# Loading x in two parts and the later weights after the first stage, in a two-layer cross-attention and feed-forward kernel

## The reference

```
x = x + L0_xattn(layernorm(x), ctx, ctx, ...)     # 16 heads of 16, softmax over 375 keys
x = x + L0_ffn(layernorm(x), ...)                 # 32 routed experts + 8 empty ones, top 6 of 40
x = x + L1_xattn(layernorm(x), ctx, ctx, ...)
x = x + L1_ffn(layernorm(x), ...)                 # gate, up, down, weights and inputs rounded to fp4 by blocks of 16
```

## Time and profile before

| | |
|---|---|
| runs | 1001.34, 998.26, 998.67 us; median 998.67 |
| profiled execution | 1005.61 us, of which the span of instructions 1003.8 us |
| TensorE busy | 898.1 us (89%) |
| VectorE busy | 626.4 us (62%) |
| ScalarE busy | 437.4 us (44%) |
| GpSimd busy | 304.1 us (30%) |
| mean granted TensorE clock | 0.951 of full |
| DMA | 90.45 MB, mean 90 GB/s |

### The profile page before, as it was taken

How to read it: one execution, slowest core, us unless ns; L and a number is a source line. 1 busy time by engine, 2 the same in 40 slices (tenths; PEclk the granted TensorE clock), 3 DMA queues, 4 the chain that set the end, 5 groups by cost and what they waited for, 6 DMA issues and landing times.

```text
span 1003.8 us, 19829 instructions
## 1 busy us (share of the span) xinstructions
PE 898.1 (89%) x7228; PEld 685.1 (68%) x7228; DVE 626.4 (62%) x1317; ACT 437.4 (44%) x946; POOL 304.1 (30%) x311
## 2 busy tenths in 40 slices
PE   2997799999997978999999967799999996699996
PEld 1764687878876747878888844587878874366664
DVE  3455577878854594545545465566777764678872
ACT  0442466666664561111111112466666675345442
POOL 8003466767782260000000004000000001476673
PEclk9998799999998798999999977999999999999998
DMA  9788644444333469121111204345565500000000
GB/s 258 219 238 203 113 93 92 93 93 93 62 106 98 138 214 250 46 67 32 32 32 48 65 3 82 74 85 112 107 117 109 106 27 21 0 11 16 16 10 22
DMA packets 98157, 90.45 MB, mean 90 GB/s; under 512 B 43554, under 2 KB 85410, under 8 KB 97954
## 3 DMA queue, kind: packets, MB, share of 16 engines
q1 hardware_dynamic: 98066, 89.25, 36.6%
HBM read 69.36 MB, written 19.63 MB: 89 GB/s over the span
## 4 chain that ended last, share of the span: by engine, by line
PE 72%; DVE 12%; DMA 5%; POOL 3%; ACT 3%; issue 2%; SPq 2%; DVEq 0%; POOLq 0%; ACTq 0%
PE ps L988 13%; PE ps L805 8%; PE ps L859 8%; PE ps L791 8%; PE ps L994 7%; PE ps L819 7%; PE ps L1062 3%; DMA Qz<-mT 3%; PE ps L709 3%; PE ps L1078 2%; PE ps L868 2%; POOL Pr L645 2%; PE ps L779 2%; PE ps L828 1%; DMA X<-x_in 1%
## 5 line engine op out<-in xcount | busy, mean ns | idle before, releaser
L1444 DVE TENSOR_REDUCE ext<-ps 112x2 f32<-112x750 f32 x256 | 232.6, 933 | 66.5 <-PE ps L791 63.4
L1175 ACT ACTIVATE Pr<-ps 125x448 f32<-125x448 f32 x384 | 199.2, 542 | 88.5 <-PE ps L805 75.0
L805 PE MATMUL ps<-Qz,Kp 98*125 98x224 f16 x768 | 130.7, 265 | 14.0 <-DMA Qz<-mT 11.7
L791 PE MATMUL ps<-Kp,Qz 96*112 96x375 f16 x512 | 122.6, 332 | 5.8 <-DMA Qz<-qscr 4.9
L805 PEld LDWEIGHTS ps<-Qz,Kp 98*125 98x125 f16 x768 | 94.8, 137 | 47.2 <-DMA Qz<-mT 15.9
L859 PE MATMUL ps<-wv,ctx 128*125 128x256 f32 x384 | 120.7, 400 | 1.9 <-DVE xT L1417 1.0
L599 POOL TENSOR_TENSOR X<-X,bo 112x256 f32 x32 | 22.5, 724 | 284.6 <-DVE Pr L1362 233.0
L1585 DVE TENSOR_TENSOR Pr<-Pr,ps 128x336 f32<-128x336 f32 (+2 forms) x86 | 32.7, 381 | 88.9 <-ACT Pr L1257 73.8
L819 PE MATMUL ps<-Pr,Vx 125*32 125x112 f32 x3072 | 86.9, 261 | 0.0
L819 PEld LDWEIGHTS ps<-Pr,Vx 125*32 125x32 f32 x3072 | 71.4, 110 | 14.9 <-ACT Pr L1175 10.3
L1589 DVE SCALAR_TENSOR_TENSOR X<-ps,W,X 112x256 f32<-112x256 f32 x167 | 70.7, 477 | 17.3 <-PE ps L994 17.3
(11 more groups left out here) (176 smaller groups left out, 1417.1 us busy)
## 6 DMA issues: line engine op xcount, KB each, us to landing
ctx<-ctxT SPq DMA_DIRECT2D x56, 375.0 KB, 3.7
Kp<-kscr SPq DMA_DIRECT2D x96, 187.5 KB, 4.8
kscr<-ksp SPq DMA_DIRECT2D x24, 375.0 KB, 4.2
Pr<-wexp SPq DMA_DIRECT2D x20, 384.0 KB, 4.2
Qz<-qscr SPq DMA_DIRECT2D x174, 28.0 KB, 4.1
expert<-wexp SPq DMA_DIRECT2D x12, 384.0 KB, 3.9
Pr<-ctxT SPq DMA_DIRECT2D x8, 375.0 KB, 4.5
kscr<-Pr SPq DMA_DIRECT2D x8, 375.0 KB, 3.9
```

What stands on the lines that cost most here:

```text
L791: last = mm(ps[0:S, 2 * (p % 2) + u, 0:M], Qz[0:96, q0 + u * S:q0 + (u + 1) * S], Kp[0:96, k0:k0 + M], start=True, stop=True)
L805: last = mm(ps[0:KC, 4 + k % 2, u * 2 * S:(u + 1) * 2 * S], Kp[0:98, k0:k0 + KC], Qz[0:98, q0:q0 + 2 * S], start=True, stop=True)
L1175: A(Pr[g % 2][0:KC, j, GI * t:GI * t + GI, :].rearrange("r h q -> r (h q)"), ps[0:KC, 4 + k % 2, 0:GI * S], ACT.Exp, scale=scale).then_inc ...
L1444: V.tensor_reduce(ext[0:S, 2 * p:2 * p + 2], ps[0:S, 2 * (p % 2):2 * (p % 2) + 2, 0:M], AX_X, red).then_inc(row_maximum_taken, 1)
```

## The change

- SP first issues the key weights and biases of layer 0, context 0, a quarter of x (4 sequences, 448 KB), context 1, the query weights, the rest of x (12 sequences, 1,344 KB), and the four other loads of layer 0.
- The other 15 loads (3,327 KB) are issued once, right after `flatten(0)` of layer 0, the `fq` weights first.
- TensorE and ScalarE start on key weights and biases alone. TensorE waits for the query weights before its first query projection.
- VectorE computes statistics of 4 sequences, normalises three, then waits for the rest of x and computes the statistics of the other 12, and only then enters the loop with `split_low(0)`.
- `scale_weights` runs one sequence later: nothing at b = 0, piece b - 1 at b, and both of the last two pieces at b = 15. The wait for `fq` moves from the first row maximum to b = 1.
- Readers of the layer-1 and router weights wait for `late_weights_loaded`.

```diff
-        NW0, NW = 16 * 3, 16 * (4 + 7 + 3)
+        NWK, NW, NL = 16 * 2, 16 * 4, 16 * (7 + 3)
+        XA = 4
...
             weight(wk[0], attn[0]["wk"], first_weights_loaded)
+            sp.dma_start(bqk[0][:, :], attn[0]["bqk"]).then_inc(first_weights_loaded, 16)
             load_ctx(0, 0)
-            sp.dma_start(X[:, :], x).then_inc(x_loaded, 16)
-            weight(wq[0], attn[0]["wq"], first_weights_loaded)
-            sp.dma_start(bqk[0][:, :], attn[0]["bqk"]).then_inc(first_weights_loaded, 16)
+            sp.dma_start(X[:, 0:XA * D], x[:, 0:XA * D]).then_inc(x_loaded, 16)
             load_ctx(1, 1)
-            for l in (0, 1):
...
+            weight(wq[0], attn[0]["wq"], query_weights_loaded)
+            sp.dma_start(X[:, XA * D:], x[:, XA * D:]).then_inc(x_rest_loaded, 16)
...
+            load_attention_weights(0, weights_loaded)
+
+            def load_late_weights():
+                for n, w in enumerate((fg, fu)):
+                    sp.dma_start(fq[:, 6 * D * n:6 * D * n + 5 * D].rearrange("p (t d) -> p t d", d=D),
+                                 w[0:640, :].rearrange("(t p) d -> p t d", p=128)).then_inc(ffn_weights_loaded, 16)
+                    sp.dma_start(fq[0:64, 6 * D * n + 5 * D:6 * D * (n + 1)], w[640:704, :]).then_inc(ffn_weights_loaded, 16)
+                sp.dma_start(fq[:, 12 * D:12 * D + 2 * FI].rearrange("p (t d) -> p t d", d=FI),
+                             fd.rearrange("(t p) d -> p t d", p=128)).then_inc(ffn_weights_loaded, 16)
+                weight(wq[1], attn[1]["wq"], late_weights_loaded)
+                weight(wk[1], attn[1]["wk"], late_weights_loaded)
+                sp.dma_start(bqk[1][:, :], attn[1]["bqk"]).then_inc(late_weights_loaded, 16)
+                load_attention_weights(1, late_weights_loaded)
+                sp.dma_start(wc_sb[:, :, :], wc.rearrange("(c p) o -> p c o", p=128)).then_inc(late_weights_loaded, 16)
+                sp.dma_start(eb_sb[:, :], ebias.partition_broadcast(128)).then_inc(late_weights_loaded, 16)
+                sp.dma_start(pow_sb[:, :], powers).then_inc(late_weights_loaded, 16)
...
                 flatten(0)
+                if l == 0:
+                    load_late_weights()
...
-                norms(False, 0, B if l == 0 else QG)
+                norms(False, 0, XA if l == 0 else QG)
...
                     layer_norm(2, xn[0]).then_inc(x_normalised, 1)
-                    dve.wait_ge(first_weights_loaded, NW0)
+                    dve.wait_ge(first_weights_loaded, NWK)
+                    dve.wait_ge(x_rest_loaded, 16)
+                    norms(False, XA, B)
...
-                if l == 0:
-                    dve.wait_ge(ffn_weights_loaded, 16 * 5)
-                    dve.wait_ge(padding_set, 7)
...
-                        elif step == "q" and l == 0:
-                            scale_weights(b, next(steps))
+                        elif step == "q" and l == 0 and b > 0:
+                            k = next(steps)
+                            if b == 1 and k == 0:
+                                dve.wait_ge(ffn_weights_loaded, 16 * 5)
+                                dve.wait_ge(padding_set, 7)
+                            scale_weights(b - 1, k)
+                            if b == B - 1 and k == 2:
+                                for k in range(3):
+                                    scale_weights(B - 1, k)
```

More of the change, by code:

```diff
@@ L215, in build @@
         first_weights_loaded = sem("first_weights_loaded")
+        query_weights_loaded = sem("query_weights_loaded")
+        late_weights_loaded = sem("late_weights_loaded")
+        x_rest_loaded = sem("x_rest_loaded")
         x_loaded = sem("x_loaded")
@@ L397, in _, with load_attention_weights @@
-            sp.dma_start(fq[:, 12 * D:12 * D + 2 * FI].rearrange("p (t d) -> p t d", d=FI),
-                         fd.rearrange("(t p) d -> p t d", p=128)).then_inc(ffn_weights_loaded, 16)
+            weight(wq[0], attn[0]["wq"], query_weights_loaded)
+            sp.dma_start(X[:, XA * D:], x[:, XA * D:]).then_inc(x_rest_loaded, 16)
+            def load_attention_weights(l, done):
+                weight(wv[l], attn[l]["wv"], done)
+                weight(wo[l], attn[l]["wo"], done)
+                sp.dma_start(bv_sb[l][:, :], attn[l]["bv"]).then_inc(done, 16)
+                sp.dma_start(bo_sb[l][:, :], attn[l]["bo"].partition_broadcast(128)).then_inc(done, 16)
```

25 lines of the change are left out of this document (7 added, 18 removed).

## The result

The changed kernel takes **1015.9 us** (median of 4 runs, 1014.5 to 1017.4), beside 1000.0 for the kernel before on the same chip: ratio 1.0156, interval 1.0124 to 1.0188. The forecast was 1000.7 with a range to 1004.5, so the kernel is slower by 1.6%, and outside the range.

What follows compares the result with a forecast made beforehand. The prediction took TensorE to hold most of the chain of waits, except through the first 30 us. Its terms, -5.4 + 2.8 + 2.4 + 2.2 = +2.0, gave 1000.7 us for the median, range 994.6 to 1004.5.

Steps and rivals of the forecast that it cites:

- Term 1: The start: third sequence's keys 8.1 us earlier, less 2.7 for a cold clock; -5.4 us (ends -7.5 and -3.5).
- term 4: Router's root chain: GpSimd's quantising, a sequence later, holds VectorE's short links; +2.2 us (0.8 to 3.4).
- the start doesn't do what it says: Rival at the start: the rest of x lands at 16.6, sum +3.6, 1002.3 us; chance 0.10.
- Term 2: Queue at `flatten(1)`: its few bytes wait behind the late loads, delaying sequence 1's columns; +2.8 us (0.5 to 5.9).
- SyncE's rival: Queue at `flatten(1)`: the 15 issues stall as at the start; sum +5.7, 1004.4 us; chance 0.15.
- Term 3: TensorE's clock behind the 3.8 us gap at sequence 1's columns falls to half; +2.4 us (0 to 3.05).
- Edits at nothing: Waits for `fq` and other late weights, and VectorE's three short instructions moved to b = 15, cost nothing.

Runs made afterwards that it cites:

- start_scale_late: start_alone with the scales of the expert weights computed one sequence later; ratio 1.0032 to the kernel before.
- start_alone: The kernel before with only the new start (x in two loads, two sets of statistics), late loads and scales in their old places; ratio 1.0020.
- after_spread: The changed kernel with five late loads kept behind `flatten(0)` and the ten others behind the flattenings of sequences 1 to 4; 1.0061 of the kernel before.
- late_alone: The kernel before with only the moved late loads and later scales, keeping the old start; ratio 1.0114.
- start_ctx_first: start_alone with 32-bit memsets, the keys' one after the third normalisation, and sequence 2's context ahead of the late loads; 0.9936 of the kernel before.
- after_memset_cover: The changed kernel with GpSimd's memsets as 32-bit words, the keys' one waiting until the third sequence is normalised; 1.0066 of the kernel before.

## Why the prediction was wrong, point by point

**Term 1, -5.4 us; it was +3.9.** This is the step that failed, and in it the sentence "the first quarter of x no longer matters: its statistics and the first two sequences are done before the rest is". I timed the early chain by its undisturbed links, while GpSimd's memset of 10.09 us stood in the trace of before at just that time, 10.71 to 20.80. I used the very mechanism in term 4, on GpSimd's 1.61 us instructions. I did not ask it of the place to which the chain was moved, where a link of 0.17 us took 10.12. The Trainium skill, page "SBUF — State Buffer", section "Who interferes with whom", says that whichever of VectorE and GpSimd takes their shared ports first holds them for its whole instruction, and names `tensor_scalar` among the VectorE instructions that can want them. The trace agrees: the held links of the start are `tensor_scalar`, and `bn_stats` beside the same memset kept 0.33 us. The arithmetic from the landing of the rest of x was right: with the memset away, 25.20 against 24.1, and 5.8 us against 5.4. The rival "the start doesn't do what it says" had a late x as its cause, at 0.10 and up to +3.6. Its sign was right, its cause wrong: the rest of x landed at 15.3 to 16.2 where it could be seen. Of the 3.9 us, 1.7 are the clock at the third keys, and that part is not sure to come: TensorE was idle 2.93 us there and restarted at 1.2 GHz, but with nearly the same start it was idle 2.82 in start_scale_late and 2.39 in start_alone and stayed at 2.4. (A slip beside it: the lower end of the term, -7.5, comes out of its own figures as -7.1, for a landing at 13.5 and 2.5 of clock.)

**Term 2, +2.8; it was +4.9.** The wait was the one I named, and the fifteen issues took 8.6 us, far from the 14.1 of SyncE's rival. Yet a part of that rival held, which I had put at nothing: with the ten issues behind them SyncE reached `flatten(1)` 1.8 us after its maxima were there. Mis-sized besides was what comes behind the loads. I let the context, keys and queries take the 5.8 us that they had taken in an empty queue and gave the flattening 0.65 more. In fact they were issued until 122.31, their many small packets kept the DMA engines full at only 150 to 230 GB/s from 122 on, the next context load joined at 123.58, and the 7 KB needed 5.96 us. My upper end of 5.9 held it, though for the most part for another reason.

**Term 3, +2.4; it was 2.2 to 2.9.** Right: 2.9 in the piece behind the columns, 2.2 as the way to the router (4.9 over the plain one) less term 4's 2.7. after_spread shows it as a thing of the gap, since it goes to 0 there. The prediction's remark that every gap is followed by half clock was too wide: the one of 1.02 us at 120.10 was not the earlier trace rows, nor were those of 2.39 and 2.69 us in later kernels.

**Term 4, +2.2; it was +2.7.** Right, and start_scale_late has it by itself. Four held links (0.64, 1.53, 1.44, 1.47) cost 4.4 us over 0.17 each; the two of the kernel before (0.53 and 1.57) cost 1.8; the difference is 2.6. I had counted one more block in place of the old ones at the low end, and every one at the high end; it was two more, one of them partly.

**Edits at nothing.** They were. No wait for late weights shows in the profile, and the scales of sequence 1 found theirs.

**The sum.** 3.9 + 4.9 + 2.2 + 2.7 = 13.7 us at the router, against +2.0: of the 11.7 us of error, 9.3 are term 1's. The ratios of the halves, with 2 us of noise each, share it out less unevenly: start_alone +2.0 against -5.4, late_alone +11.4 against +7.4, and 2.2 that neither half shows. Of the two repairs, the memset is worth 9 to 10 us by the ratios and the spreading 9.5.

**Left open.** In the kernels with the new start and early loads the step from sequence 0 to 1 is 12.7 to 13.6 us where the kernel before has 14.6. The traces show two things in it: TensorE's clock is back at 2.4 GHz 3.9 us after the columns of sequence 0 in start_alone and 4.5 in start_ctx_first, against 6.1 before, and TensorE waits 0.28 and 0.50 us for the columns of sequence 1 instead of 1.02. No experiment says why the clock comes back sooner. Nor can I say why the memset on VectorE in the whole change (1.0054) is not worse than under cover (1.0066), although its start is 2.6 us later; the intervals overlap.

## What to carry to other kernels

When work is moved earlier, look up what every other engine does at the new place in time, setup work too: a memset that nobody waits for can cost its whole length as soon as a neighbour's short instructions of the kind held here come beside it. Before moving large loads away from the start, see which one smaller load stands behind them; moving that one ahead gave 0.5% here, while moving the large ones, with the later scales that this asked for, cost 1.1% by itself. And an earlier step is worth its full distance only if the next one in line is early too, since the engine that waits for it loses part of the gain at half clock (in after_memset_cover the third keys came 7.0 us sooner, the fourth 5.3).

## What the runs showed of the hardware

- A 112x4 VectorE instruction on 32-bit integers and one on fp32 (`tensor_scalar` both) were each held for a whole GpSimd memset, 10.1 us; sixteen `bn_stats` beside the same memset kept 0.33 us each.
- A memset's time goes by elements per partition and not by bytes: 12000 fp16 numbers took 10.09 us, the same bytes as 6000 32-bit words 5.09. VectorE took 10.06 for the fp16 form, no less than GpSimd (while GpSimd ran another memset).
- Small transfers can wait for large ones that another engine's queue issued: 3.5 KB took 9.5 to 10.1 us to land while ScalarE's 3.41 MB were under way (240 to 310 GB/s in all), where the same kind took 1.7 to 2.3 us in start_alone.
- TensorE's clock fell to 1.2 GHz after an idle gap of 2.79 us in one kernel and held at 2.4 GHz after 2.69 us at the same place in another.
